# Second attention and feed-forward stage: the quantised second layer moved behind the last exp, two tiles in a turn

## The chip, the cores and the metric

One core of one Trainium2 chip runs the whole program. The metric is the device time of one execution in microseconds (us). Engines are named as in the profile: PE is TensorE, with PEld for its weight loads, DVE is VectorE, ACT is ScalarE, POOL is GpSimd, SP is SyncE, which here only issues DMAs.

## The reference

The reference is four blocks in a row, each added to x with a tanh gate: a perceiver cross-attention, a mixture-of-experts block, a second cross-attention, and a feed-forward block with quantised linear layers. x is 32 x 64 x 128, that is 2048 rows of 128, or NT = 16 tiles of 128 rows. The change lies in the last two blocks, and there in the feed-forward:

```
def act_quant(x):
    scale = 127.0 / clip(max(abs(x), axis=-1), EPS)
    return clip(round(x * scale), -128, 127), scale
...
h = layernorm(x, gamma, beta)          # rows of 128
h = qlinear(h, w1, b1)                 # ternary weights, 128 -> 512
h = gelu(h, approximate=False)
out = qlinear(h, w2, b2)               # quantised again by row, 512 -> 128
```

The second cross-attention (`_L1_xattn_ref`) has 16 heads of 8 and 64 keys for each batch element, so it takes one exp over 16 x 64 scores for each row. The feed-forward takes one gelu over 512 values for each row.

## The kernel before

The program runs in stages one after the other; the last stage, `attention_ffn`, does the last two blocks. It is a software pipeline over the 16 tiles, written out by hand for each engine. Each engine has a loop over turns `s`, and in turn `s` it does one step each for several tiles: for instance ScalarE in turn s does `exp(s - 2)` (line 1609) and `norm_out(s - 5)` (line 1624), VectorE does `row_max(s)` (line 1689), `shift(s - 1)` (line 1694), `attend(s - 2)` (lines 1702 and 1708), `output(s - 2)` (line 1717), `norm_round(s - 4)` (line 1745) and `hidden(s - 5)` (line 1752). Every engine takes its instructions strictly in the order written; semaphores tie the engines together. Whatever stands behind a waiting instruction on its engine waits as well.

The steps of one tile are: turn and project the context and the input on TensorE; `scores` (line 1448) into the four banks `p_s`; row maximum, `shift`, `exp`; `probs_T` (line 1463) turns the probabilities, ScalarE copies them out (`probs_out`, line 1614), `mix` (line 1478) weighs the values; `attend`, `turn_attention`, `attention_out`, `out_proj` and `output` finish the attention. GpSimd normalises the new row, `norm_round` quantises it, `up` (line 1513) is the first ternary layer, and `hidden` scales it back and adds the bias into `hid`, 128 x 512 float32.

The second layer of a tile t is then: `gelu` (ScalarE, line 1628, in place in `hid`), `hidden_largest` (VectorE, row maximum, line 1758), `hidden_factors` (lines 1763 and 1766), `hidden_round` (line 1770), `turn_hidden` (TensorE, four transposes into bank `p_t`, line 1521), `hidden_out` (ScalarE, to bf16, line 1633), `down` (TensorE, four matmuls into `p_y`, line 1530), and `final` (VectorE, line 1777), with `hidden_back` and `add_bias_2` (GpSimd, lines 1387 and 1392) before it. SyncE stores two tiles at a time after `final` (line 1341).

`exp` and `gelu` need different tables of ScalarE, and a table load goes in front of the first of each after the other. So the gelus are taken in groups: `GROUPS` (line 1273) names tiles 0-3, 4-7, 8-11, 12-13 and 14-15, and the gelus of a group run in the turn after the last of its tiles is ready, at the head of ScalarE's turn. `hid` is a ring of eight tiles. The other steps of the second layer lag behind: `hidden_largest` to `hidden_round` run for tile s - 9, `turn_hidden` for s - 11, `down` and `final` for s - 12. `busy` (line 53, its matmuls on line 57) issues matmuls with no use but to keep TensorE at work. `BUSY` (line 1274) puts such calls ahead of `scores` for a few tiles, 5 before tile 9 and 2 before tile 13 among them, and from turn 18 on each turn of TensorE begins with 3 of them, in the lines quoted here. One call is two matmul instructions in the profile.

```
for s in range(NT + 12):
    if s >= NT + 2:
        wait(pe, shifted, NT)
        busy(nc, p_s[:, 0, 0:256], ident[:], v["wq_a"][:, 0:256], 3)
```

Of the kernel before, what the change touches and what calls it, by code (L numbers as in the profile page):

```python
# [22 lines left out]
ALU = mybir.AluOpType  # L23
# [1235 lines left out]
def attention_ffn(nc, v, o_tiles):  # L1259

    xs, cs, moments, neghalf, ident, quad = (v[n] for n in "xs cs moments neghalf ident quad".split())
# [8 lines left out]
    RING = 8  # L1272
    GROUPS = ((0, 4), (4, 8), (8, 12), (12, 14), (14, 16))
    BUSY = {0: 3, 1: 3, 2: 2, 3: 1, 9: 5, 13: 2}
    with ExitStack() as ph, nc.Block() as block:
# [27 lines left out]
        hid = sb("hid", [P, RING, FF])  # L1303
        gT = sb("gT", [P, 2, C, P], BF16)
# [4 lines left out]
        xb2 = sb("xb2", [P, 2, D])  # L1309
# [8 lines left out]
        p_prob, p_mix = (p_m, p_t), (p_m, p_y)  # L1318
# [18 lines left out]
        @block.sync  # L1337
        def _(sp):
            for t in range(NT // 2):
                sp.wait_ge(x_done, 2 * t + 2)  # L1340
                sp.dma_start(o_tiles[:, 2 * t:2 * t + 2, :], xs[:, 2 * t:2 * t + 2, :]).then_inc(stored, 16)
            sp.wait_ge(stored, 16 * (NT // 2))

        @block.gpsimd
        def _(pool):
# [38 lines left out]
            def hidden_back(t):  # L1384
                pool.wait_ge(g_bound, t + 1)
                wait(pool, x_done, t - 3)
                nc.gpsimd.tensor_tensor(back_[:, 1, t % 4], top[:, 1, t % 4], wback[:, 1:2], ALU.mult).then_inc(g_back, 1)

            def add_bias_2(t, tp):
                pool.wait_ge(x_new, t + 1)  # L1390
                wait(pool, x_done, t - 1)
                nc.gpsimd.tensor_tensor(xb2[:, tp, :], xs[:, t, :], rows[:, 3, :], ALU.add).then_inc(xb2_ready, 1)

            pool.wait_ge(ready, 1)
            for s in range(NT + 13):
# [4 lines left out]
                if exists(s - 13, NT):  # L1400
                    add_bias_2(s - 13, (s - 13) % 2)
# [5 lines left out]
                if exists(s - 12, NT):  # L1407
                    hidden_back(s - 12)
# [4 lines left out]
        def _(pe):  # L1413
# [38 lines left out]
            def probs_T(t, tp, j):  # L1452
# [4 lines left out]
                else:  # L1457
                    pe.wait_ge(cT_ready, min(t + 3, NT))
                    wait(pe, gT_ready, t - 8)
# [7 lines left out]
            def mix(t, tp, j):  # L1467
                pe.wait_ge(prT_ready, 2 * t + j + 1)
                pe.wait_ge(v_ready, 2 * t + 2)
                if j == 1:  # L1470
                    wait(pe, x_new, t)
                    wait(pe, hid_ready, t - 3)
                    wait(pe, x_done, t - 9)
# [18 lines left out]
            def out_proj(t, tp):  # L1492
                pe.wait_ge(oT_ready, t + 1)
                wait(pe, hid_ready, t - 2)
                wait(pe, x_done, t - 9)
# [11 lines left out]
            def up(t, tp):  # L1507
# [4 lines left out]
                wait(pe, x_done, t - 6)  # L1512
                nc.tensor.matmul(p_y[:], hT[:, tp, :], w1_t[:], start=True, stop=True).then_inc(up_done, 1)  # L1513

            def turn_hidden(t):
                pe.wait_ge(g_rounded, t + 1)
                pe.wait_ge(cT_ready, min(t + 12, NT))
                pe.wait_ge(prT_ready, min(2 * t + 18, 2 * NT))
                wait(pe, gT_ready, t)
                for c in range(C):  # L1520
                    last = nc.tensor.transpose(p_t[:, c * P:(c + 1) * P], hid[:, t % RING, c * P:(c + 1) * P], ident[:])  # L1521
                last.then_inc(gT_done, 1)

            def down(t, tp):
                pe.wait_ge(gT_ready, t + 1)
                pe.wait_ge(x_new, min(t + 10, NT))
                pe.wait_ge(hid_ready, min(t + 7, NT))
                wait(pe, x_done, t)
                for c in range(C):
                    last = nc.tensor.matmul(p_y[:, 0:D], gT[:, tp, c, :], w2_t[:, c, :], start=(c == 0), stop=(c == C - 1))  # L1530
# [12 lines left out]
            for s in range(NT + 12):  # L1543
                if s >= NT + 2:
                    wait(pe, shifted, NT)
                    busy(nc, p_s[:, 0, 0:256], ident[:], v["wq_a"][:, 0:256], 3)
# [10 lines left out]
                if exists(s - 11, NT):  # L1557
                    turn_hidden(s - 11)
                if exists(s, NT):
                    turn_input(s, s % 2)  # L1560
                if exists(s - 6, NT):
                    up(s - 6, s % 2)
                if exists(s - 3, NT):
# [12 lines left out]
                if exists(s - 12, NT):  # L1576
                    down(s - 12, s % 2)

        @block.scalar
        def _(act):  # L1580
# [45 lines left out]
            def gelu(t):  # L1626
# [214 lines left out]
```

## Time and profile before

| | us |
|---|---|
| median of 3 runs | 463.04 |
| lowest and highest run | 460.96, 463.33 |
| the profiled execution | 460.61 |
| its span, first to last instruction | 458.8 |
| busy in the span: PE, DVE, ACT, POOL | 412.8, 338.7, 263.3, 234.6 |

The span is what the trace covers; 1.8 us of the execution's own time lie around it. The last stage runs from about 304 us to the end. Times in the timeline and in the chain are from the span's start. The granted clock is TensorE's: 1.00 is 2.4 GHz, 0.50 is 1.2 GHz, and a value between is a stretch with both. In the chain of waits each piece is what the piece after it waited for.

### The profile page before, as it was taken

To read this page: it belongs to the slowest core of one execution; us is meant where nothing else is said; L and a number is where in the kernel's file an instruction comes from. 1 tells how busy PE (TensorE), PEld (TensorE's weight loads), DVE (VectorE), ACT (ScalarE), POOL (GpSimd) and SP (SyncE) were. 2 spreads that over 40 slices of the span, in tenths; PEclk is the share of its full clock that TensorE was granted. 3 is DMA by queue.
4 is the path that set the end of the run, shared out by engine and by line. 5 is a ranking of instruction groups with operands and counts; after the bars stand their busy time and mean duration, and the time that the engine had idled before them with its cause. 6 is when DMAs were issued, how large, how long until landed. Compare 5 with 4: busy or idle time off the path is not lost. (4 is left out here: it accounts for less than half of the span.)

```text
span 458.8 us, 11161 instructions
## 1 busy us (share of the span) xinstructions
PE 412.8 (90%) x3810; PEld 307.2 (67%) x3810; DVE 338.7 (74%) x965; ACT 263.3 (57%) x543; POOL 234.6 (51%) x404
## 2 busy tenths in 40 slices
PE   4698999999999999878899989988888979898877
PEld 4355666666666666756788878865666756666656
DVE  3689888888888888865577745553478859879674
ACT  1266777777777776712522244416667768875542
POOL 3545656666666666350300034444388848666621
PEclk8689999999999999999999999989999989988899
DMA  5889999000000000000000000000000000000001
GB/s 166 246 117 120 130 130 106 2 2 2 1 1 3 1 1 2 1 3 0 2 1 0 0 1 2 1 0 2 1 1 3 2 1 1 14 2 15 12 24 34
DMA packets 61285, 13.30 MB, mean 29 GB/s; under 512 B 51488, under 2 KB 60592, under 8 KB 61232
## 3 DMA queue, kind: packets, MB, share of 16 engines
q1 hardware_dynamic: 59776, 11.94, 18.5%
q10 hardware_dynamic: 1328, 0.66, 0.5%
q8 instruction: 32, 0.52, 0.5%
q14 instruction: 21, 0.17, 0.1%
q0 software_dynamic: 128, 0.00, 0.0%
HBM read 11.55 MB, written 1.05 MB: 27 GB/s over the span
## 5 line engine op out<-in xcount | busy, mean ns | idle before, releaser
L332 POOL TENSOR_TENSOR a_rn<-a_ssq,neghalf 128x8 f32<-128x8 f32 x48 | 79.2, 1653 | 25.7 <-DVE a_ssq L682 18.1
L682 DVE TENSOR_REDUCE a_ssq<-a_sq 128x8 f32<-128x512 f32 x48 | 32.4, 675 | 16.1 <-ACT a_sq L539 15.9
L1689 DVE TENSOR_REDUCE b_mx<-b_s 128x16 f32<-128x1024 f32 x16 | 19.6, 1223 | 22.5 <-PE b_s L1448 22.5
L409 PE MATMUL a_x<-wkv_a,a_kvT 128*128 128x512 f32 x64 | 35.3, 634 | 0.5 <-ACT a_kvT L532 0.5
L57 PE MATMUL b_s<-wq_a,ident 128*128 128x256 f32 x106 | 31.9, 448 | 3.1 <-PEq L1139 2.2
L545 ACT ACTIVATE a_vaug<-a_x,maskcol 128x512 f32<-128x512 f32 x32 | 21.9, 683 | 17.8 <-PE a_x L409 17.8
L1355 POOL TENSOR_TENSOR b_k<-b_ksb,quad 128x256 f32<-128x256 f32 x32 | 19.1, 618 | 21.9 <-ACT b_ksb L1595 21.8
L1163 POOL COPY c_staged<-eo_T 128x256 f32<-128x256 f32 x16 | 6.2, 391 | 45.3 <-SPq L1139 44.2
L57 PEld LDWEIGHTS b_s<-wq_a,ident 128*128 128x128 f32 x106 | 22.7, 228 | 6.8 <-issue 2.4
L1100 ACT ACTIVATE e_hg<-e_g 128x512 f32<-128x512 f32 x16 | 9.6, 597 | 28.9 <-PE e_g L1068 28.9
L701 DVE TENSOR_REDUCE a_mx<-a_s 128x4 f32<-128x512 f32 x32 | 22.0, 687 | 3.1 <-PE a_s L435 3.1
L348 POOL TENSOR_TENSOR a_yr<-a_ymv,eps_row 128x1 f32<-128x1 f32 x16 | 3.0, 189 | 41.1 <-DVE a_ymv L725 41.1
L557 ACT ACTIVATE a_kT<-a_m,cols 128x512 f32<-128x512 f32 x32 | 21.9, 686 | 1.4 <-PE a_m L423 1.3
L423 PEld LDWEIGHTS a_m<-ident,a_kn 128*128 128x128 f32 x128 | 15.8, 143 | 9.6 <-issue 8.8
L454 PE MATMUL a_m<-a_vaug,a_prT 128*64 128x65 f32 x512 | 21.9, 228 | 0.3 <-ACT a_prT L567 0.3
L445 PEld LDWEIGHTS a_m<-ident,a_pr 128*128 128x128 f32 x128 | 14.6, 140 | 11.1 <-issue 10.0
L708 DVE TENSOR_TENSOR a_pr<-a_s,a_mx 128x512 f32<-128x512 f32 x32 | 21.9, 684 | 0.0
L435 PEld LDWEIGHTS a_s<-a_kT,a_qT 64*64 64x64 f32 x512 | 13.8, 132 | 12.0 <-issue 12.0
L473 PEld LDWEIGHTS a_y<-wo_a,a_attT 128*128 128x128 f32 x128 | 16.6, 191 | 7.3 <-issue 7.2
L454 PEld LDWEIGHTS a_m<-a_vaug,a_prT 128*64 128x64 f32 x512 | 17.6, 137 | 5.6 <-issue 5.6
L567 ACT COPY a_prT<-a_m 128x512 f32<-128x512 f32 x32 | 18.8, 586 | 4.1 <-PE a_m L445 4.1
L445 PE MATMUL a_m<-ident,a_pr 128*128 128x128 f32 x128 | 20.1, 280 | 0.9 <-ACT a_pr L562 0.9
(254 smaller groups left out, 1237.2 us busy)
## 6 DMA issues: line engine op xcount, KB each, us to landing
w_gu<-in_L_ffn_Wg_dram SPq DMA_DIRECT2D x4, 512.0 KB, 8.7
w_gu<-in_L_ffn_Wu_dram SPq DMA_DIRECT2D x4, 512.0 KB, 11.1
w_d<-in_L_ffn_Wd_dram SPq DMA_DIRECT2D x8, 256.0 KB, 8.1
out_dram<-xs SPq DMA_DIRECT2D x8, 128.0 KB, 1.8
xs<-in_x_dram SPq DMA_DIRECT2D x1, 640.0 KB, 11.4
cs<-in_ctx_dram SPq DMA_DIRECT2D x1, 640.0 KB, 11.8
wkv_a<-in_L_xattn_Wkv_dram SPq DMA_DIRECT2D x1, 512.0 KB, 7.8
nat<-in_L_ffn_w_dram SPq DMA_DIRECT2D x2, 256.0 KB, 2.9
```

The costliest lines, as they stand in the source:

```text
L57: nc.tensor.matmul(bank, weights, moving, start=True, stop=True)
L332: nc.gpsimd.tensor_tensor(rn[:, tp, i, :], ssq[:, tp, i, :], neghalf[:, 0:H0], ALU.pow)\
L409: nc.tensor.matmul(p_x[:], kvT[:, tp, b * 2 * S:(b + 1) * 2 * S], wkv_a[:, INNER:2 * INNER], start=True, stop=True).then_inc(vproj_done, 1)
L445: last = nc.tensor.transpose(p_m[a][:, h * P:(h + 1) * P], pr[:, a, h, :], ident[:])
L454: last = nc.tensor.matmul(p_m[a][b * S:(b + 1) * S, h * W:(h + 1) * W], prT[:, a, h, b * S:(b + 1) * S], vaug[:, tp, b, 2 * h + a, :], sta ...
L545: nc.scalar.activation(vaug[:, tp, b, :, 0:DH0], p_x[:].rearrange("p (h d) -> p h d", h=H0), ACT.Copy, scale=maskcol[:, 2 * t + b:2 * t + ...
L557: nc.scalar.activation(kT[:, tp, b, :, :], p_m[b][:].rearrange("p (h k) -> p h k", h=HP), ACT.Copy, scale=cols[:, 4:5]).then_inc(kT_ready, 1)
L682: nc.vector.tensor_reduce(ssq[:, tp, i, :], sq[:, i, :].rearrange("p (h d) -> p h d", h=H0), AX.X, ALU.add).then_inc(reduced, 1)
L701: nc.vector.tensor_reduce(mx[:, a, :], p_s[a][:].rearrange("p (h k) -> p h k", h=HP), AX.X, ALU.max)\
L708: nc.vector.tensor_tensor(pr[:, a], s3, mx[:, a, :].unsqueeze(2).to_broadcast([P, HP, P]), ALU.subtract).then_inc(shifted, 1)
L1355: last = nc.gpsimd.tensor_tensor(k4[:, tp, b], ksb[:, tp, b].unsqueeze(1).to_broadcast([P, G, S]), quad[:].unsqueeze(2).to_broadcast([P, G ...
L1689: nc.vector.tensor_reduce(mx[:, tp], s4, AX.X, ALU.max).then_inc(maxed, 1)
```

## The change

All gelus and the whole second layer move behind the last `exp`, and are done for two tiles (a pair j, of NP = 8) in a turn. ScalarE does `gelu(j)` in turn 17 + j, right behind `exp` and ahead of its copies, and `hidden_out(j)` at the end of turn 18 + j. VectorE does `hidden_largest(j)`, `hidden_bound(j)` and `hidden_factor(j)` in turn 17 + j, its two `hidden_round` in turn 18 + j, and `final(j)` in turn 20 + j, between `hidden_largest` and the rounds. TensorE does `down(j)` in turn 20 + j and behind it `turn_hidden(j + 1)`; so `turn_hidden(j)` is in turn 19 + j. The eight transposes of a pair go into two of the four banks `p_s`, whose last scores are gone by then, and the two products into `p_t` or `p_m`. `hid` holds all 16 tiles. Two calls of `busy` stand in each `turn_hidden`, ahead of its wait for the rounded rows; the calls for tiles 9 and 13 and those at the head of the late turns are gone, and so are the waits on the second layer in `mix`, `probs_T`, `out_proj`, `up` and `hidden`. The second bias is added in place in `xs`, for two tiles at once.

```
-    RING = 8
-    GROUPS = ((0, 4), (4, 8), (8, 12), (12, 14), (14, 16))
-    BUSY = {0: 3, 1: 3, 2: 2, 3: 1, 9: 5, 13: 2}
+    NP = NT // 2
+    BUSY = {0: 3, 1: 3, 2: 2, 3: 1}
...
-        hid = sb("hid", [P, RING, FF])
-        gT = sb("gT", [P, 2, C, P], BF16)
+        hid = sb("hid", [P, NT, FF])
+        gT = sb("gT", [P, 2, 2, C, P], BF16)
...
-        p_prob, p_mix = (p_m, p_t), (p_m, p_y)
+        p_prob, p_mix, p_out = (p_m, p_t), (p_m, p_y), (p_t, p_m)
...
-                sp.wait_ge(x_done, 2 * t + 2)
+                sp.wait_ge(x_done, t + 1)
...
-            def hidden_back(t):
-                pool.wait_ge(g_bound, t + 1)
-                wait(pool, x_done, t - 3)
-                nc.gpsimd.tensor_tensor(back_[:, 1, t % 4], top[:, 1, t % 4], wback[:, 1:2], ALU.mult).then_inc(g_back, 1)
-            def add_bias_2(t, tp):
-                pool.wait_ge(x_new, t + 1)
-                wait(pool, x_done, t - 1)
-                nc.gpsimd.tensor_tensor(xb2[:, tp, :], xs[:, t, :], rows[:, 3, :], ALU.add).then_inc(xb2_ready, 1)
+            def add_bias_2(j):
+                pool.wait_ge(x_new, 2 * j + 2)
+                pool.wait_ge(mv_ready, 2 * j + 2)
+                r = slice(2 * j, 2 * j + 2)
+                nc.gpsimd.tensor_tensor(xs[:, r, :], xs[:, r, :], rows[:, 3, :].unsqueeze(1).to_broadcast([P, 2, D]),
+                                        ALU.add).then_inc(xb2_ready, 1)
+            def hidden_back(j):
+                pool.wait_ge(g_bound, j + 1)
+                wait(pool, x_done, j - 1)
+                r = slice(2 * (j % 2), 2 * (j % 2) + 2)
+                nc.gpsimd.tensor_tensor(back_[:, 1, r, 0], top[:, 1, r, 0], wback[:, 1:2].to_broadcast([P, 2]),
+                                        ALU.mult).then_inc(g_back, 1)
 
             pool.wait_ge(ready, 1)
-            for s in range(NT + 13):
+            for s in range(NT + 4 + NP):
                 if exists(s - 4, NT):
                     add_bias(s - 4, s % 2)
                 if exists(s - 7, NT):
                     norm_back(s - 7)
-                if exists(s - 13, NT):
-                    add_bias_2(s - 13, (s - 13) % 2)
                 if exists(s - 3, NT):
                     spread_keys(s - 3, (s - 3) % 2)
                 if exists(s - 6, NT):
                     inverse_root(s - 6)
                     norm(s - 6, s % 2)
-                if exists(s - 12, NT):
-                    hidden_back(s - 12)
+                if exists(s - NT - 4, NP):
+                    hidden_back(s - NT - 4)
+                    add_bias_2(s - NT - 4)
...
-            def turn_hidden(t):
-                pe.wait_ge(g_rounded, t + 1)
-                pe.wait_ge(cT_ready, min(t + 12, NT))
-                pe.wait_ge(prT_ready, min(2 * t + 18, 2 * NT))
-                wait(pe, gT_ready, t)
-                for c in range(C):
-                    last = nc.tensor.transpose(p_t[:, c * P:(c + 1) * P], hid[:, t % RING, c * P:(c + 1) * P], ident[:])
+            def turn_hidden(j):
+                if j < 2:
+                    pe.wait_ge(shifted, NT)
+                wait(pe, gT_ready, j - 1)
+                busy(nc, p_s[:, 2 * (j % 2), 0:256], ident[:], v["wq_a"][:, 0:256], 2)
+                pe.wait_ge(g_rounded, 2 * j + 2)
+                for i in range(2):
+                    for c in range(C):
+                        last = nc.tensor.transpose(p_s[:, 2 * (j % 2) + i, c * P:(c + 1) * P],
+                                                   hid[:, 2 * j + i, c * P:(c + 1) * P], ident[:])
                 last.then_inc(gT_done, 1)
 
-            def down(t, tp):
-                pe.wait_ge(gT_ready, t + 1)
-                pe.wait_ge(x_new, min(t + 10, NT))
-                pe.wait_ge(hid_ready, min(t + 7, NT))
-                wait(pe, x_done, t)
-                for c in range(C):
-                    last = nc.tensor.matmul(p_y[:, 0:D], gT[:, tp, c, :], w2_t[:, c, :], start=(c == 0), stop=(c == C - 1))
+            def down(j):
+                pe.wait_ge(gT_ready, j + 1)
+                if j == 0:
+                    pe.wait_ge(prT_ready, 2 * NT)
+                if j == 1:
+                    pe.wait_ge(att_ready, NT)
+                wait(pe, x_done, j - 1)
+                for i in range(2):
+                    for c in range(C):
+                        last = nc.tensor.matmul(p_out[j % 2][:, i * P:(i + 1) * P], gT[:, j % 2, i, c, :], w2_t[:, c, :],
+                                                start=(c == 0), stop=(c == C - 1))
                 last.then_inc(down_done, 1)
...
-            for s in range(NT + 12):
-                if s >= NT + 2:
-                    wait(pe, shifted, NT)
-                    busy(nc, p_s[:, 0, 0:256], ident[:], v["wq_a"][:, 0:256], 3)
+            for s in range(NT + 4 + NP):
                 if exists(s - 1, 2):
                     turn_ternary(s - 1)
                 if s == 3:
@@ -1554,12 +1557,14 @@
                     project(s - 1, (s - 1) % 2)
                 if exists(s - 3, NT):
                     mix(s - 3, (s - 3) % 2, 1)
-                if exists(s - 11, NT):
-                    turn_hidden(s - 11)
                 if exists(s, NT):
                     turn_input(s, s % 2)
                 if exists(s - 6, NT):
                     up(s - 6, s % 2)
+                if exists(s - NT - 4, NP):
+                    down(s - NT - 4)
+                if exists(s - NT - 3, NP):
+                    turn_hidden(s - NT - 3)
...
-                if exists(s - 12, NT):
-                    down(s - 12, s % 2)
...
-            def gelu(t):
-                act.wait_ge(hid_ready, t + 1)
-                nc.scalar.activation(hid[:, t % RING, :], hid[:, t % RING, :], ACT.Gelu).then_inc(gelu_done, 1)
-            def hidden_out(t, tp):
-                act.wait_ge(gT_done, t + 1)
-                wait(act, down_done, t - 1)
-                nc.scalar.activation(gT[:, tp].rearrange("p c k -> p (c k)"), p_t[:], ACT.Copy, bias=-MAGIC)\
-                    .then_inc(gT_ready, 1)
+            def gelu(j):
+                act.wait_ge(hid_ready, 2 * j + 2)
+                pair = hid[:, 2 * j:2 * j + 2, :].rearrange("p t k -> p (t k)")
+                nc.scalar.activation(pair, pair, ACT.Gelu).then_inc(gelu_done, 1)
+            def hidden_out(j):
+                act.wait_ge(gT_done, j + 1)
+                wait(act, down_done, j - 1)
+                nc.scalar.activation(gT[:, j % 2].rearrange("p i c k -> p (i c k)"),
+                                     p_s[:, 2 * (j % 2):2 * (j % 2) + 2, :].rearrange("p i k -> p (i k)"),
+                                     ACT.Copy, bias=-MAGIC).then_inc(gT_ready, 1)
...
-            for s in range(NT + 11):
+            for s in range(NT + 2 + NP):
                 if s == 2:
                     ternary_out(0, w1_t[:])
                 if s == 3:
                     ternary_out(1, w2_t[:].rearrange("p c k -> p (c k)"))
-                for first, end in GROUPS:
-                    if s - 7 == end - 1:
-                        for t in range(first, end):
-                            gelu(t)
                 if exists(s, NT):
                     context_out(s, s % 2)
                 if exists(s - 1, NT):
                     projections_out(s - 1, (s - 1) % 2)
                 if exists(s - 2, NT):
                     exp(s - 2, s % 2)
+                if exists(s - NT - 1, NP):
+                    gelu(s - NT - 1)
                 if exists(s, NT):
                     input_out(s, s % 2)
-                if exists(s - 11, NT):
-                    hidden_out(s - 11, (s - 11) % 2)
...
+                if exists(s - NT - 2, NP):
+                    hidden_out(s - NT - 2)
...
-            def hidden_largest(t):
-                dve.wait_ge(gelu_done, t + 1)
-                wait(dve, g_back, t - 3)
-                nc.vector.tensor_reduce(top[:, 1, t % 4], hid[:, t % RING, :], AX.X, ALU.max, apply_absolute_value=True)\
-                    .then_inc(g_max, 1)
-            def hidden_factors(t):
-                dve.wait_ge(g_max, t + 1)
-                nc.vector.tensor_scalar(top[:, 1, t % 4], top[:, 1, t % 4], EPS, 1.0 / 127.0, ALU.max, ALU.mult)\
+            def pair(j):
+                return slice(2 * (j % 2), 2 * (j % 2) + 2)
+            def hidden_largest(j):
+                dve.wait_ge(gelu_done, j + 1)
+                wait(dve, g_back, j - 1)
+                nc.vector.tensor_reduce(top[:, 1, pair(j), 0], hid[:, 2 * j:2 * j + 2, :], AX.X, ALU.max,
+                                        apply_absolute_value=True).then_inc(g_max, 1)
+            def hidden_bound(j):
+                dve.wait_ge(g_max, j + 1)
+                nc.vector.tensor_scalar(top[:, 1, pair(j), 0], top[:, 1, pair(j), 0], EPS, 1.0 / 127.0, ALU.max, ALU.mult)\
                     .then_inc(g_bound, 1)
-                dve.wait_ge(g_bound, t + 1)
-                nc.vector.reciprocal(fine[:, 1, t % 4], top[:, 1, t % 4]).then_inc(g_fine, 1)
+            def hidden_factor(j):
+                dve.wait_ge(g_bound, j + 1)
+                nc.vector.reciprocal(fine[:, 1, pair(j), 0], top[:, 1, pair(j), 0]).then_inc(g_fine, 1)
 
             def hidden_round(t):
-                dve.wait_ge(g_fine, t + 1)
-                nc.vector.tensor_scalar(hid[:, t % RING, :], hid[:, t % RING, :], fine[:, 1, t % 4], MAGIC,
+                dve.wait_ge(g_fine, t // 2 + 1)
+                nc.vector.tensor_scalar(hid[:, t, :], hid[:, t, :], fine[:, 1, t % 4], MAGIC,
                                         ALU.mult, ALU.add).then_inc(g_rounded, 1)
 
-            def final(t, tp):
-                dve.wait_ge(down_done, t + 1)
-                dve.wait_ge(xb2_ready, t + 1)
-                dve.wait_ge(g_back, t + 1)
-                nc.vector.scalar_tensor_tensor(xs[:, t, :], p_y[:, 0:D], back_[:, 1, t % 4], xb2[:, tp, :],
-                                               ALU.mult, ALU.add).then_inc(x_done, 1)
-            for s in range(NT + 12):
+            def final(j):
+                dve.wait_ge(down_done, j + 1)
+                dve.wait_ge(xb2_ready, j + 1)
+                dve.wait_ge(g_back, j + 1)
+                for i in range(2):
+                    last = nc.vector.scalar_tensor_tensor(xs[:, 2 * j + i, :], p_out[j % 2][:, i * P:(i + 1) * P],
+                                                          back_[:, 1, (2 * j + i) % 4], xs[:, 2 * j + i, :],
+                                                          ALU.mult, ALU.add)
+                last.then_inc(x_done, 1)
+            for s in range(NT + 4 + NP):
                 if exists(s - 3, NT):
                     row_stats(s - 3, (s - 3) % 2)
-                if exists(s - 12, NT):
-                    final(s - 12, s % 2)
                 if exists(s - 1, NT):
                     shift(s - 1, (s - 1) % 2)
                 if exists(s - 3, NT):
                     row_moments(s - 3, (s - 3) % 2)
                 if exists(s - 2, NT):
                     attend(s - 2, s % 2)
-                if exists(s - 9, NT):
-                    hidden_largest(s - 9)
+                if exists(s - NT - 1, NP):
+                    hidden_largest(s - NT - 1)
                 if exists(s - 4, NT):
                     norm_round(s - 4, s % 2)
-                if exists(s - 9, NT):
-                    hidden_factors(s - 9)
+                if exists(s - NT - 4, NP):
+                    final(s - NT - 4)
+                if exists(s - NT - 2, NP):
+                    hidden_round(2 * (s - NT - 2))
+                if exists(s - NT - 1, NP):
+                    hidden_bound(s - NT - 1)
                 if exists(s - 5, NT):
                     hidden(s - 5)
-                if exists(s - 9, NT):
-                    hidden_round(s - 9)
+                if exists(s - NT - 2, NP):
+                    hidden_round(2 * (s - NT - 2) + 1)
+                if exists(s - NT - 1, NP):
+                    hidden_factor(s - NT - 1)
...
```

## Rows read from the trace of the kernel before

**Rows 1.** The page of the profiled execution, its head

```profile
span 458.8 us, 11161 instructions
```

**Rows 2.** Timeline of ScalarE: start, duration, engine, line, operation, idle before it.

```profile
343.60 1.06 ACT L1609 ACTIVATE b_pr<-b_pr 128x1024 f32<-128x1024 f32 x1
...
361.78 1.06 ACT L1609 ACTIVATE b_pr<-b_pr 128x1024 f32<-128x1024 f32 x1
...
380.01 1.06 ACT L1609 ACTIVATE b_pr<-b_pr 128x1024 f32<-128x1024 f32 x1
...
393.08 1.06 ACT L1609 ACTIVATE b_pr<-b_pr 128x1024 f32<-128x1024 f32 x1
...
396.57 1.28 ACT L1628 ACT_TABLE_LOAD   x1
397.87 2.19 ACT L1628 ACTIVATE b_hid<-b_hid 128x512 f32<-128x512 f32 x4
...
409.82 1.06 ACT L1609 ACTIVATE b_pr<-b_pr 128x1024 f32<-128x1024 f32 x1
...
422.40 1.06 ACT L1609 ACTIVATE b_pr<-b_pr 128x1024 f32<-128x1024 f32 x1 [2.57 <-DVE b_pr L1694]
```

**Rows 3.** Busy time of the engines in five stretches, with the granted clock.

```profile
core 0: us, PE busy (x) PEld busy (x) DVE busy (x) ACT busy (x) POOL busy (x), PEclk, DMA share, GB/s
343.60:361.80 18.20, 15.85 (x213) 12.11 (x213) 15.69 (x44) 13.05 (x34) 14.86 (x31) 1.00 0.01 3
418.00:422.00 4.00, 2.78 (x47) 2.44 (x47) 3.78 (x10) 1.68 (x5) 2.89 (x7) 1.00 0.00 0
422.00:425.50 3.50, 3.50 (x19) 2.80 (x16) 3.13 (x12) 2.49 (x4) 2.62 (x6) 0.51 0.03 7
428.00:432.00 4.00, 2.81 (x27) 1.63 (x25) 3.04 (x11) 2.98 (x7) 2.45 (x6) 1.00 0.11 33
432.20:435.40 3.20, 3.19 (x11) 2.55 (x12) 1.78 (x8) 0.00 (x0) 2.13 (x5) 0.51 0.00 0
```

**Rows 4.** The chain that ended last, its last stage: start, duration, what.

```profile
422.14 1.04 PE b_t L1521 x4
...
448.57 1.35 PE b_s L57 x6
449.93 0.44 PE b_t L1521 x4
450.36 0.22 PE b_y L1530 x4
...
456.22 0.35 DVE xs L1777
```

**Rows 5.** Timeline of all engines in the tail: start, duration, engine, line, operation.

```profile
429.26 0.21 DVE L1708 TENSOR_TENSOR b_att<-b_y,b_rs 128x64 f32<-128x64 f32 x1
...
443.17 0.75 DVE L1752 SCALAR_TENSOR_TENSOR b_hid<-b_y,b_back_,b1row 128x512 f32<-128x512 f32 x1 [0.67 <-PE b_y L1513]
...
443.83 0.48 DVE L1770 TENSOR_SCALAR b_hid<-b_hid,b_fine 128x512 f32<-128x512 f32 x1
444.14 0.24 PEld L1530 LDWEIGHTS b_y<-w_t,b_gT 128*128 128x128 bf16 x4 [1.40 <-ACT b_gT L1633]
...
450.40 0.60 ACT L1633 ACTIVATE b_gT<-b_t 128x512 bf16<-128x512 f32 x1 [1.41 <-PE b_t L1521]
```

**Rows 6.** Groups of the last stage by shape: busy, mean ns, idle before.

```profile
L1689 DVE TENSOR_REDUCE b_mx<-b_s 128x16 f32<-128x1024 f32 x16 | 19.6, 1223 | 22.5 <-PE b_s L1448 22.5
...
L1355 POOL TENSOR_TENSOR b_k<-b_ksb,quad 128x256 f32<-128x256 f32 x32 | 19.1, 618 | 21.9 <-ACT b_ksb L1595 21.8
...
L1758 DVE TENSOR_REDUCE b_top<-b_hid 128x1 f32<-128x512 f32 x16 | 10.8, 674 | 0.0
...
L1614 ACT COPY b_prT<-b_t 128x512 f32<-128x512 f32 x16 | 9.5, 592 | 0.2 <-PE b_t L1463 0.2
```

**Rows 7.** The instructions of line 1770: durations in ns, min/median/max, first and last start.

```profile
L1770 DVE TENSOR_SCALAR b_hid<-b_hid,b_fine x16: 476/479/794, 369.5 to 452.0; 128x512 f32<-128x512 f32 x16
```

More of the change, by code:

```diff
@@ L1308, in attention_ffn @@
         wback = sb("wback", [P, 2])
-        xb2 = sb("xb2", [P, 2, D])
         wscale = sb("wscale", [P, 2])
@@ L1458, in probs_T @@
                     pe.wait_ge(cT_ready, min(t + 3, NT))
-                    wait(pe, gT_ready, t - 8)
                     wait(pe, prT_ready, 2 * t)
@@ L1472, in mix @@
                     wait(pe, hid_ready, t - 3)
-                    wait(pe, x_done, t - 9)
                     wait(pe, att_ready, t)
@@ L1494, in out_proj @@
                 wait(pe, hid_ready, t - 2)
-                wait(pe, x_done, t - 9)
                 nc.tensor.matmul(p_y[:, 0:D], oT[:, tp, :], w_c[:, 3, :], start=True, stop=True).then_inc(y_done, 1)
@@ L1511, in up @@
                 wait(pe, hid_ready, t)
-                wait(pe, x_done, t - 6)
                 nc.tensor.matmul(p_y[:], hT[:, tp, :], w1_t[:], start=True, stop=True).then_inc(up_done, 1)
-            def turn_hidden(t):
-                pe.wait_ge(g_rounded, t + 1)
-                pe.wait_ge(cT_ready, min(t + 12, NT))
-                pe.wait_ge(prT_ready, min(2 * t + 18, 2 * NT))
-                wait(pe, gT_ready, t)
-                for c in range(C):
-                    last = nc.tensor.transpose(p_t[:, c * P:(c + 1) * P], hid[:, t % RING, c * P:(c + 1) * P], ident[:])
-                last.then_inc(gT_done, 1)
-            def down(t, tp):
-                pe.wait_ge(gT_ready, t + 1)
-                pe.wait_ge(x_new, min(t + 10, NT))
-                pe.wait_ge(hid_ready, min(t + 7, NT))
-                wait(pe, x_done, t)
-                for c in range(C):
-                    last = nc.tensor.matmul(p_y[:, 0:D], gT[:, tp, c, :], w2_t[:, c, :], start=(c == 0), stop=(c == C - 1))
+            def turn_hidden(j):
[8 more added lines that the diff above has]
+                                                   hid[:, 2 * j + i, c * P:(c + 1) * P], ident[:])
+                last.then_inc(gT_done, 1)
+            def down(j):
[9 more added lines that the diff above has]
+                                                start=(c == 0), stop=(c == C - 1))
                 last.then_inc(down_done, 1)
@@ L1750, in hidden @@
                 dve.wait_ge(h_back, t + 1)
-                wait(dve, gT_done, t - RING + 1)
-                nc.vector.scalar_tensor_tensor(hid[:, t % RING, :], p_y[:], back_[:, 0, t % 4], b1row[:],
+                nc.vector.scalar_tensor_tensor(hid[:, t, :], p_y[:], back_[:, 0, t % 4], b1row[:],
                                                ALU.mult, ALU.add).then_inc(hid_ready, 1)
-            def hidden_largest(t):
-                dve.wait_ge(gelu_done, t + 1)
-                wait(dve, g_back, t - 3)
-                nc.vector.tensor_reduce(top[:, 1, t % 4], hid[:, t % RING, :], AX.X, ALU.max, apply_absolute_value=True)\
-                    .then_inc(g_max, 1)
```

## The prediction

> **What bounds the kernel now.** I read four views, and only for the last stage, since the change touches no other. The span is 458.8 us [rows 1], and the profiled execution took 460.61, so 1.8 lie around the span. The sum below is made against this execution; it is 2.4 us (0.5%) under the median of 463.04. About 0.5% is also what a measurement of this kernel can tell from no change.
>
> The timeline of ScalarE [rows 2] gives the pace. From the exp at 343.60 to that at 361.78 lie three turns: 6.06 us each, with TensorE busy 15.85 of 18.20 us at a granted clock of 1.00 [rows 3]. From there to the exp of the last tile at 422.40 lie eight turns in 60.62 us, or 7.6 each. The reader is to see where the excess over 6.06 sits: 6.1 us in the two turns to 380.01 (the first group of gelus and the cold turn behind it), 1.0 in the two turns to 393.08 (the first `down`), 4.6 in the two to 409.82 (a load of 1.28, four gelus in 2.19, and a second load, all ahead of ScalarE's copies), 0.5 in the last two. Together 12.1.
>
> After the last exp comes the tail, 34.2 us from 422.40 to the end of the last `final` at 456.57 [rows 2, 4]; the store of the last rows takes 2.2 more. The chain of waits there is all TensorE: for a tile 1.35 of `busy`, 0.44 of four transposes, 0.22 of `down`, 2.01 in sum [rows 4]. The filler sets the pace, and the rest hides behind it.
>
> **What the change takes away.** The eight turns lose the gelus, four of the six table loads, the two extra fillers and the second layer. What is left is the turn of 343.60 to 361.78, which already ran without any of these and stayed at clock 1.00. So the last exp starts at 361.78 + 8 x 6.06 = 410.3, a gain of 12.1. Transposes and row work that leave these turns give nothing beyond this: the turn of 6.06 was paced without them. The waits on the second layer that go from `mix`, `probs_T`, `out_proj` and `up` are priced at nothing of their own, since in the turn of 6.06 they did not yet wait for anything. SyncE keeps its eight stores; each goes as soon as its pair is done, and only the last counts, 2.2 as before.
>
> **What it adds: a ring through four engines.** In the tail I wrote down, engine by engine, the order of the instructions. VectorE in turn 18 + j: `hidden_largest(j+1)`, `final(j-2)`, round, bound, round of pair j. The row maximum needs `gelu(j+1)`. ScalarE takes `gelu(j+1)` only behind `hidden_out(j-1)`, the last item of its turn before. That needs `turn_hidden(j-1)`, and that the rounds of pair j-1, the turn before on VectorE. So from round to round everything stands in one line, with two tiles for each trip. The new wait of `hidden_out` at the head of ScalarE's queue is the knot: the next gelu is ready to run, and is queued behind it.
>
> One trip, step by step:
> - VectorE to TensorE 0.22: a `hidden` of 0.75 started at 443.17, so it ended at 443.92, and the weight load that it let go started at 444.14 [rows 5].
> - Eight transposes: four are 0.44 in the chain [rows 4], the last result about 0.16 later; 8 x 0.11 + 0.16 = 1.04.
> - TensorE to ScalarE 0.03 (chain piece ends 450.37, `hidden_out` starts 450.40), then `hidden_out` over 1024 elements. 512 took 0.60 and the exp over 1024 took 1.06 [rows 2, 5], so 1.05.
> - `gelu(j+1)`, the pair in one instruction: four of 512 took 2.19 [rows 2], 0.53 for each further one, so 1.06, less 0.08 of overlap: 0.98, and 0.05 to VectorE.
> - `hidden_largest` over 1024: 512 took 0.674, and the row maximum over 1024 from PSUM 1.223 [rows 6]. VectorE starts the next instruction 0.09 before one ends (443.17 + 0.75 against 443.83 [rows 5]), so 1.13.
> - `final` twice, 0.35 each [rows 4], 0.27 in a row: 0.54. First round 0.40, bound 0.16 (estimate from the smallest operations), second round 0.48 [rows 7].
>
> Sum: 0.22 + 1.04 + 0.03 + 1.05 + 0.98 + 0.05 + 1.13 + 0.54 + 0.40 + 0.16 + 0.48 = 6.1 us for a pair, where two tiles took 4.02. Off the ring lie `down`, `busy`, factor, GpSimd and the stores: TensorE does `down` and the filler while it would wait.
>
> Two terms the trace of before does not show as such. **GpSimd beside the rounds:** `final` lets `hidden_back` and `add_bias_2` go, the latter over 256 elements, about 0.6 us like line 1355 [rows 6], and they fall on the rounds. Line 1770 took 479 ns as a rule and up to 794 [rows 7]. The bounds are 0 and 0.3 for each of two rounds; I take 0.16 for a trip. The Trainium skill, SBUF — State Buffer, "Who interferes with whom", says that VectorE in a two-port mode and GpSimd exclude each other for a whole instruction. By this rule the price would be the whole rest of a GpSimd instruction each time; the spread of line 1770 agrees with it.
>
> **TensorE's clock:** in a trip of 6.1 us TensorE has some 2.7 us of work: 1.04 of transposes, 0.6 of `down`, 1.0 of filler, 44% busy. In 418.0 to 422.0 it was busy 2.78 of 4.00 us, and 422.0 to 425.5 then ran at 0.51; in 428 to 432 it was 2.81 of 4.00, and 432.2 to 435.4 ran at 0.51 [rows 3]. Both were busier than a trip of the ring. So I expect 1.2 GHz for most of the tail. There four transposes take 1.04 on the chain in place of 0.44 [rows 4]; twice that difference is 1.2 for eight. I take +0.8, since the piece of 1.04 holds the start of the first transpose, which eight pay once; the ends are 0 and +1.2. The Trainium skill, TensorE: Matmul & The Clock Gate, Part 4, says that transposes do not count as work for the clock in the way that matmuls do. By that the tail is at 1.2 GHz whatever the two fillers do. The turns at clock 1.00, with a dozen transposes each, show that they at least do not prevent it.
>
> **The tail in full,** from the last exp at 410.3, cold values in brackets.
> - Up to the end of `attend` for the last tile: exp 1.06, load 1.28, gelu(0) 1.06, `attention_out` 0.3, two `probs_out` 1.1 (line 1614, 592 ns [rows 6]), `mix` 0.65, `attend` 0.65: 6.1. These stand in line, as gelu(0) is ahead of the copies. Before, `attend` ended 7.1 after the exp [rows 2, 5], so the load hurts little here.
> - Two turns of VectorE with a row maximum, `hidden`, the norm's and the output's work each, about 3.3 (3.13 to 3.78 us of its work stood in 3.5 to 4.0 before [rows 3]): 6.6. The rounds of pair 0 are done at 410.3 + 12.7 = 423.0.
> - Six trips: 36.6, plus two `hidden` and a norm left over (1.5), less one `final` (0.5), plus 1.0 for GpSimd: 38.6 (+4.9).
> - Behind the sixth: transposes, `hidden_out`, `down`, filler, transposes of pair 7, `hidden_out`, `down`, two `final`: 7.5 (10.4).
>
> So the last `final` ends at 423.0 + 38.6 + 7.5 = 469.1, or 476.9 cold. With the store's 2.2 and 1.8 around the span: 473.1, or 480.9. The tail has become 59 to 67 us in place of 34.2, against 12.1 gained. I take 480, the cold case with a few trips at full clock.
>
> **Rivals.**
> - *The tail stays at 2.4 GHz*, as the fillers mean it to: 473. For it: eight pieces of work in a trip leave no long gap. Against: the two stretches above. Chance 0.25.
> - *The steps overlap, and it is faster.* If the rounds of a pair did not stand behind the next row maximum, a trip would be VectorE's own work, 2.7 + 0.16, or 2.9 us, the six trips 19.4, and the time 473.1 - 19.2 = 454. The point from which this decides is a trip of 4.2 us: 12.7 + 6 x 4.2 + 1.0 + 7.5 = 46.4 = 34.2 + 12.1. The ring is 1.9 above it, and only an error in the order of a queue, not in a duration, could bring it there. Chance 0.04. The Trainium skill, ScalarE: Activation LUTs, "Table sets: the hidden batching unit", asks for just this change: all calls of one table set together. By the rule alone, four loads of 1.28 us, about 5 us, are gained; the trace agrees that each load is there, and it is inside the 12.1.
> - *The change does only part of what it says:* without the second layer the turns do not fall to 6.06, because something else, such as the clock, holds them at 6.7. Then 480 + 5 = 485. Against: the three turns at 1.00. Chance 0.1.
> - The forecast itself, 480 within 3: 0.61.
>
> **Range and chances.** Warm and cold tail are 473 and 481; the unknown costs add 2 below (lead-in) and 4 above (transposes, GpSimd), and the slow turns reach 485. I give 471 to 488. Faster by over 0.5%: 0.04. Within 0.5%: 0.02. Slower: 0.94.
>
> **What would show it.** Right: exps 6.1 apart up to one at about 410; then `hidden_out` 6 to 7 us apart, each row maximum starting right behind a gelu, each gelu right behind a `hidden_out`, ScalarE idle until TensorE's transposes and VectorE idle until the gelu, TensorE at 0.50 or little more from about 425 on. Wrong: pairs 3 to 4 us apart with VectorE busy throughout; or exps that keep 6.7 and more; or a chain with `busy` on it in the tail.

## The result and the profile after

The changed kernel takes 479.29 us (median of 4 runs, 478.68 to 479.61), against 462.00 for the kernel before in the same comparison: a ratio of 1.0376, 95% interval 1.0331 to 1.042. The forecast was 480, in a range of 471 to 488. Ratios, here and below, are of the means of the executions, without the few that fell in a slower state of the chip; the times given are medians. The profiled execution has a span of 476.9 us, and all the readings in this section are of it.

| from the start of the span, us | before | forecast | after |
|---|---|---|---|
| exp of tile 7 starts | 361.78 | 361.78 | 361.53 |
| exp of the last tile starts | 422.40 | 410.3 | 409.20 |
| its `attend` ends | 429.47 | 416.4 | 416.34 |
| rounds of pair 0 end | | 423.0 | 423.5 |
| last `final` ends | 456.57 | 469.1 warm, 476.9 cold | 474.65 |

The tail, from the start of the last exp to the end of the last `final`, takes 65.5 us in place of 34.2.

The first view is ScalarE's timeline again; it answers to [rows 2].

```profile
409.20 1.06 ACT L1612 ACTIVATE b_pr<-b_pr 128x1024 f32<-128x1024 f32 x1 [2.00 <-DVE b_pr L1697]
410.27 1.28 ACT L1632 ACT_TABLE_LOAD   x1
...
425.56 1.02 ACT L1637 ACTIVATE b_gT<-b_s 128x1024 bf16<-128x1024 f32 x1 [6.87 <-PE b_s L1522]
426.48 1.05 ACT L1632 ACTIVATE b_hid<-b_hid 128x1024 f32<-128x1024 f32 x1
...
431.99 1.02 ACT L1637 ACTIVATE b_gT<-b_s 128x1024 bf16<-128x1024 f32 x1 [4.30 <-PE b_s L1522]
...
445.16 1.02 ACT L1637 ACTIVATE b_gT<-b_s 128x1024 bf16<-128x1024 f32 x1 [4.52 <-PE b_s L1522]
...
452.37 1.02 ACT L1637 ACTIVATE b_gT<-b_s 128x1024 bf16<-128x1024 f32 x1 [5.24 <-PE b_s L1522]
453.29 1.05 ACT L1632 ACTIVATE b_hid<-b_hid 128x1024 f32<-128x1024 f32 x1
...
459.58 1.02 ACT L1637 ACTIVATE b_gT<-b_s 128x1024 bf16<-128x1024 f32 x1 [5.24 <-PE b_s L1522]
...
472.30 1.02 ACT L1637 ACTIVATE b_gT<-b_s 128x1024 bf16<-128x1024 f32 x1 [4.50 <-PE b_s L1522]
```

The last eight turns up to the exp at 409.20 take 5.96 us on average: all the excess of before is gone. From one `hidden_out` (L1637) to the next, over all eight of them, are 6.43, 6.69, 6.48, 7.21, 7.21, 7.20 and 5.52 us. ScalarE has been idle for 6.87 us ahead of the first of them and for 4.3 to 5.2 us ahead of each other one, waiting for the transposes. As soon as it has one, it takes the gelu (L1632) that stood behind.

The chain of waits shows one whole trip, from the transposes of a pair to those of the next:

```profile
450.37 1.98 PE b_s L1522 x8
452.40 0.90 issue
453.29 1.06 ACT b_hid L1632
454.37 0.06 DVE b_top L1763
454.44 1.07 issue
455.51 0.60 DVE xs L1785 x2
456.11 0.39 DVE b_hid L1777
456.50 0.08 DVE b_top L1768
456.58 0.95 DVE b_hid L1777
457.53 0.04 issue
```

Read down: transposes, `hidden_out` (the piece "issue" of 0.90, since the gelu starts 0.92 after it), gelu, row maximum (0.06 and the "issue" of 1.07), the two finals, first round, bound, second round. From 450.37 to the next transposes at 457.57 are 7.20. TensorE, ScalarE and VectorE are on it in turn, and each stands idle while the others work. In the kernel before, the chain lay on TensorE alone only from 444.2 on; in the 15 us ahead of that VectorE's `hidden` (L1752, 0.76 each) stood on it as well.

In the first trip the ring was not what came last. The filler of TensorE was, behind `down`:

```profile
428.36 0.85 PE b_t L1535 x8
429.21 1.81 PE b_s L57 x4
431.02 0.95 PE b_s L1522 x8
```

It stood on the chain once more, for 1.81 again, ahead of the transposes of the last pair (468.89), and nowhere else.

The windows view says at what clock, as [rows 3] did before:

```profile
core 0: us, PE busy (x) PEld busy (x) DVE busy (x) ACT busy (x) POOL busy (x), PEclk, DMA share, GB/s
363.60:403.85 40.25, 34.90 (x475) 27.00 (x472) 34.87 (x97) 28.47 (x74) 31.37 (x66) 1.00 0.01 2
409.20:425.50 16.30, 11.26 (x64) 8.15 (x64) 10.52 (x38) 6.38 (x10) 10.09 (x22) 0.54 0.01 2
425.50:438.70 13.20, 8.95 (x45) 6.53 (x43) 6.33 (x15) 4.30 (x7) 0.98 (x2) 0.66 0.03 11
438.70:445.20 6.50, 2.79 (x20) 1.95 (x20) 3.21 (x7) 1.98 (x3) 0.98 (x2) 0.96 0.07 20
445.20:472.30 27.10, 18.85 (x80) 14.25 (x80) 11.55 (x27) 6.90 (x7) 4.16 (x8) 0.51 0.09 25
```

The attention turns stay at 1.00. The tail is at 0.54, 0.66, 0.96 and 0.51; in the stretch at 0.96 the pair took 6.48, in the last one a full trip took 7.2.

### The profile page after: what moved, and what is told of

The parts are those of the page before. It is cut to its first block and busy times, and to the rows that moved or that the text cites. A ratio compares the mean times of both kernels' runs of the same rounds, so it can differ in the third digit from the quotient of the medians.

```text
span 476.9 us, 10923 instructions
## 1 busy us (share of the span) xinstructions
PE 413.4 (87%) x3768; PEld 305.4 (64%) x3768; DVE 339.3 (71%) x941; ACT 257.3 (54%) x523; POOL 232.6 (49%) x388
## 5 line engine op out<-in xcount | busy, mean ns | idle before, releaser
L1637 ACT ACTIVATE b_gT<-b_s 128x1024 bf16<-128x1024 f32 x8 | 8.2, 1024 | 40.4 <-PE b_s L1522 40.4
L1354 POOL TENSOR_TENSOR b_k<-b_ksb,quad 128x256 f32<-128x256 f32 x32 | 19.0, 614 | 19.2 <-ACT b_ksb L1598 19.2
L57 PE MATMUL b_s<-wq_a,ident 128*128 128x256 f32 x64 | 23.0, 504 | 3.1 <-PEq L1139 2.2
L1763 DVE TENSOR_REDUCE b_top<-b_hid 128x2 f32<-128x1024 f32 x8 | 9.7, 1214 | 21.1 <-ACT b_hid L1632 21.1
```

The source lines that it names most:

```text
L57: nc.tensor.matmul(bank, weights, moving, start=True, stop=True)
L1354: last = nc.gpsimd.tensor_tensor(k4[:, tp, b], ksb[:, tp, b].unsqueeze(1).to_broadcast([P, G, S]), quad[:].unsqueeze(2).to_broadcast([P, G ...
```

## The experiments

Each kernel is the changed one with the edit shown. The times are medians beside runs of the kernel before on the same chip: 461.48 us for the order of ScalarE, the five calls of `busy`, the early bias and the late `final`; 460.36 for the kernel without `busy` and for the last one of the table; 461.57 for the rest. Executions differ by some us ahead of the edits (the last exp starts between 408.7 and 414.1), so the tail of the profiled one, from the last exp's start to the end of the last `final`, is given too: it is 65.5 us in the changed kernel.

**One line on ScalarE.** `hidden_out` goes one turn later, so that it stands behind the next gelu and not ahead of it:

```
-                if exists(s - NT - 2, NP):
-                    hidden_out(s - NT - 2)
+                if exists(s - NT - 3, NP):
+                    hidden_out(s - NT - 3)
```

> Ring theory: with hidden_out(j-1) behind gelu(j+1) in place of ahead of it, the round trip spans two turns of VectorE instead of one. The pace of a pair falls from 6.4 to 7.2 us to VectorE's own work, about 3.4 (row maximum 1.13, two finals 0.6, rounds 1.4, the small ones 0.3), the chain in the tail runs over VectorE, and the kernel takes 457 to 462 us. Rival, cold clock or size of the work: the pairs are slow because TensorE is at 1.2 GHz and GpSimd stands beside the rounds, the order of ScalarE's queue is not what counts: the pace stays above 6, the time within 1% of 479.

Measured: 459.62 us, a ratio to before of 0.998 (0.9936 to 1.0025). By the medians this one line gives back 19.7 us (18 by the ratios), the whole loss of 17.3; a difference to the kernel before is not shown. The tail fell from 65.5 to 46.3. GpSimd still stands beside the second round (1.03 us) and the work in the tail is the same. TensorE's clock did rise with it, from 0.61 to 0.78 over the tail, so this run alone does not rule out the cold clock; the next one does, with a clock of 0.86 and a tail of 62.7. The pace was 3.53, and the chain of the late tail is not VectorE's, against what I expected:

```profile
438.56 1.03 ACT b_gT L1637
...
439.64 0.62 PE b_m L1535 x8
440.26 0.92 PE b_s L57 x4
441.18 0.89 PE b_s L1522 x8
442.09 1.03 ACT b_gT L1637
```

It goes from `hidden_out` (L1637) over `down` (L1535) and the filler (L57) to the next pair's transposes (L1522): a second, shorter ring, made by the order on TensorE.

**The clock.** Five calls of `busy` in `turn_hidden`, or none, in place of two (`..., 2)` becomes `..., 5)` or `..., 0)`).

> Five calls of busy in each turn_hidden in place of two. Ring theory: TensorE has idle time in each trip, so the calls cost nothing, and the granted clock stays at 1.00; the eight transposes take 1.3 in place of 2.0 us, trips become 6.45 in place of 7.2, and the last stretch of two turns shortens as well or loses a little to the longer filler: 474 to 477 us. Rival, the ring is not the limit: no gain, or the filler itself comes on the chain, 479 to 486.

> The changed kernel without the two calls of busy in turn_hidden. If they do not hold the clock, the granted clock is 0.5 in the whole tail, the trips are 7.2 us from the first to the last (a little less where the filler stood on the chain, 1.8 us in the first full trip and 1.8 in the last), and the time stays within 2 us of 479. If they do hold it in part (pairs 2 to 4 ran at 6.4 to 6.7), it is lost there: 480 to 482. A theory in which the filler itself slows the tail gives 473 or less.

Measured: 476.40 us with five (ratio to before 1.0329, 1.0242 to 1.0415; tail 62.7) and 482.12 with none (1.0455, 1.039 to 1.0521; tail 66.1). The windows, of the kernel with five and then of that with none:

```profile
core 0: us, PE busy (x) PEld busy (x) DVE busy (x) ACT busy (x) POOL busy (x), PEclk, DMA share, GB/s
425.70:439.70 14.00, 9.76 (x57) 7.92 (x55) 6.33 (x15) 4.27 (x6) 0.98 (x2) 0.88 0.03 10
439.70:469.90 30.20, 19.42 (x131) 15.51 (x130) 14.76 (x34) 8.92 (x10) 5.13 (x10) 1.00 0.09 27
```

```profile
core 0: us, PE busy (x) PEld busy (x) DVE busy (x) ACT busy (x) POOL busy (x), PEclk, DMA share, GB/s
425.00:475.00 50.00, 23.35 (x123) 18.71 (x124) 22.79 (x55) 13.16 (x15) 8.27 (x18) 0.50 0.06 16
```

With five calls the last full trips ran at 1.00 and took 6.33; with none the tail ran at 0.50 and they took 7.27. So the clock is worth about 0.9 us a trip, and the ring is there at either clock. The 5.7 us between the two kernels are not the clock's price: 2.3 of them lie ahead of the last exp (409.48 and 411.75), and the tails differ by 3.4 only, as the filler itself came on the chain with five calls. It stood there for 3.72 us in the trip from 431.92 to 439.75, which took 7.83. Two calls held the clock now and then.

**GpSimd beside the rounds.** `add_bias_2` moves into the attention turns:

```
                     norm(s - 6, s % 2)
+                if s % 2 == 1 and exists((s - 7) // 2, NP):
+                    add_bias_2((s - 7) // 2)
...
                     hidden_back(s - NT - 4)
-                    add_bias_2(s - NT - 4)
```

> add_bias_2 is done on GpSimd in the attention turns, one pair every second turn, behind the norm of its second tile, in place of the tail. If it is the instruction that holds up the second round (1.02 us in place of 0.48), the second round falls to 0.5 to 0.7, each trip by 0.3 to 0.5, six trips by 2 to 3 us: 476 to 477, unless the attention turns get longer. Rival: the second round is slow for another reason (the small product of hidden_back alone, or waiting for its own pipeline): it stays at 1.0, and the time at 479.

VectorE and GpSimd in the changed kernel, and then VectorE's rounds in this one:

```profile
448.82 0.48 DVE L1777 TENSOR_SCALAR b_hid<-b_hid,b_fine 128x512 f32<-128x512 f32 x1
449.05 0.30 POOL L1395 TENSOR_TENSOR b_back_<-b_top,b_wback 128x2 f32<-128x2 f32 x1 [5.51 <-DVE xs L1785]
...
449.28 1.03 DVE L1777 TENSOR_SCALAR b_hid<-b_hid,b_fine 128x512 f32<-128x512 f32 x1
449.31 0.72 POOL L1388 TENSOR_TENSOR xs<-xs,rows 128x256 f32<-128x256 f32 x1
```

```profile
448.60 0.47 DVE L1778 TENSOR_SCALAR b_hid<-b_hid,b_fine 128x512 f32<-128x512 f32 x1
...
449.06 0.48 DVE L1778 TENSOR_SCALAR b_hid<-b_hid,b_fine 128x512 f32<-128x512 f32 x1
```

In the first, the second round (L1777, at 449.28) takes 1.03 and ends 0.28 after GpSimd's addition does (L1388, 449.31 + 0.72); in the second it takes 0.48. The small product of `hidden_back` (L1395) is still beside the rounds there, so it is the addition that holds the second one up. That is so in four trips of the changed kernel; in the first ones `hidden` (L1754) stands between the two rounds on VectorE, and the second one, coming later, takes 0.48. The time was inconclusive: 479.04, but in four executions from 475.88 to 480.10, with mean granted clocks of 0.934 down to 0.917. In the profiled one, of 475.88, the tail was 62.3, and the later trips were 5.8 us where the clock was high and 6.7 where it was low, each 0.5 to 0.7 under those of the changed kernel. The shorter trip seems to have met the low clock more often in the others; that is not shown, as they have no trace.

**`final` behind the rounds** on VectorE (the two lines of `final` move behind `hidden_factor`).

> final(j) moves on VectorE behind the rounds and the factor, where VectorE waits for the next gelu anyway. Ring theory: every trip loses the two finals, 0.6 us, so six or seven trips give 3.5 to 4; and what final lets go on GpSimd starts behind the rounds, so the second round falls to 0.5 as well, another 3. Together 472 to 474. Rival, throughput: VectorE's work is the same and the time stays at 479.

Measured: 474.97 us (ratio 1.0287, 1.0198 to 1.0376). In the trace the trips fell to 5.3 to 5.5 us:

```profile
454.63 1.02 ACT L1637 ACTIVATE b_gT<-b_s 128x1024 bf16<-128x1024 f32 x1 [3.57 <-PE b_s L1522]
...
459.90 1.02 ACT L1637 ACTIVATE b_gT<-b_s 128x1024 bf16<-128x1024 f32 x1 [3.30 <-PE b_s L1522]
```

That is 1.7 to 1.9 less than 7.2, and more than the two terms I had named (0.6 and 0.55), since the clock came up too: 0.87 from 444 to 470. Against the 6.33 of a trip at 1.00, the 5.27 are 1.06 less, which is near the two terms. The tail took 57.4 us in place of 65.5. Half of that gain did not reach the time of this execution, as its first turns of the stage were slower, far ahead of the edit (the last exp starts at 413.69).

**The gelu behind the probabilities' copies** (the two lines of `gelu` move behind `probs_out(s - 2, 1)`).

> The changed kernel with this one edit (gelu behind the copies of the last probabilities). The ring theory says that the pace of the pairs stays at 6.4 to 7.2 us, since within a trip gelu(j+1) still stands behind hidden_out(j-1): 478 to 479. A rival, that the table load ahead of the copies is what makes the tail long, would give 474 or less.

Measured: 477.50 us (ratio 1.0376, 1.0295 to 1.0457). `attend` of the last tile ended 5.5 us after the exp's start in place of 7.1, but the trips stayed at 6.3 to 7.2. Where the load stands is not what makes the tail long.

**Breaking the rings one after the other.** On TensorE `turn_hidden(s - NT - 3)` goes ahead of `down(s - NT - 4)`, on top of the first edit; then `add_bias_2` early as well; then also the late gelu, or also the late `final`.

> As e1_order, and on TensorE turn_hidden(j+1) goes ahead of down(j). In e1_order the chain of the late tail is hidden_out(j), down(j), busy, turn_hidden(j+1), hidden_out(j+1): 1.03 + 0.05 + 0.62 + 0.92 + 0.89 = 3.53 us for a pair, a shorter ring. Ring theory: with this ring broken too, the pace falls to VectorE's own work, 3.3 us with the slow second round: only 0.2 us for a pair, some 1 to 1.5 us in all, 458 to 459. Rival: the pace of 3.53 in e1_order is VectorE's already (its steps sum to 3.3 and the rest is waiting for semaphores): no change.

> As e5_turn_first, with add_bias_2 in the attention turns. If the pace is VectorE's now, the second round's fall from 1.03 to 0.48 goes through to every pair: 2.8 to 2.9 us, some 4 to 5 us under e1_order: 454 to 456, faster than the kernel before by 1% or more. Rival: another ring of 3.4 to 3.5 us holds the pace, and the time stays at 458 to 459.

> As e6_best, with the gelu of a turn behind the copies of the last probabilities, so that the table load and gelu(0) no longer stand ahead of them. If the lead-in waits for these copies, attend of the last tile ends 1.3 to 1.5 us sooner, and the time falls by 1 us (453 to 455). Rival: the lead-in is set by VectorE's chain of two turns and by gelu(0) itself: no change, or a little slower.

> As e6_best, and final goes behind the rounds on VectorE. In e6_best the chain of the late tail is a third, shorter ring: transposes of pair j+1 1.09, down(j) 0.46, final(j) 0.61, rounds 0.87, 3.10 us with the latencies. With final behind the rounds it is broken, and what is left is VectorE's own work of 2.85 us. Ring theory: 0.25 us for each of six pairs, 1 to 1.5 in all: 453 to 454. Rival: VectorE was already within a tenth of its own work, and the last final comes later by its place: no change, 454 to 455.

| kernel | us | ratio to before | pace of a late pair | tail |
|---|---|---|---|---|
| order of ScalarE alone | 459.62 | 0.998 (0.9936 to 1.0025) | 3.53 | 46.3 |
| and `turn_hidden` first | 458.92 | 0.9943 (0.9904 to 0.9982) | 3.65 | 43.7 |
| and the bias early | 454.79 | 0.9892 (0.9805 to 0.9978) | 3.10 | 41.4 |
| and the gelu late | 455.23 | 0.9864 (0.9804 to 0.9925) | 3.10 | 40.9 |
| bias early and `final` late | 455.99 | 0.9885 (0.9843 to 0.9926) | 3.10 | 41.2 |

The third kernel is about 1% faster than the kernel before. By the times it is not clearly apart from the second, whose interval overlaps its own; its tail is 2.3 us shorter. The last three can't be told apart by their times. The pace of the third is not VectorE's own work (2.85) either; its chain:

```profile
440.74 1.09 PE b_s L1523 x8
441.83 0.46 PE b_t L1536 x8
442.32 0.61 DVE xs L1786 x2
442.93 0.40 DVE b_hid L1778
443.32 0.07 DVE b_top L1769
443.40 0.40 DVE b_hid L1778
443.84 1.09 PE b_s L1523 x8
```

Transposes (L1523), `down` (L1536), the finals that wait for it (L1786), the rounds (L1778), the next transposes: a third ring, through `final` ahead of the rounds. It was there in the kernel above it too, with the slow second round in it, 3.65; my 3.3 for that one was wrong, and its total right only because its first two trips (3.87 and 3.02 in place of 6.05 and 3.53) and its last one got shorter. Moving `final` back broke this ring, and a fourth took its place at the same 3.10, which I had not seen:

```profile
443.36 0.52 DVE xs L1786 x2
...
444.01 0.21 POOL b_back_ L1395
...
444.31 1.22 DVE b_top L1764
445.53 0.40 DVE b_hid L1778
```

`final` (L1786) lets `hidden_back` go on GpSimd (L1395), and the next row maximum (L1764) waits for that, as `top` and `back_` have room for two pairs only. More room was not tried. The late gelu brought 0.5 us of tail here, which the times do not show: `attend` ended 5.0 us after the exp's start in place of 6.2, but the row maximum then waited 0.32 for gelu(0).

## Why the prediction was right

- **The gain ahead of the tail.** Forecast: eight turns of 6.06, the last exp at 410.3. Measured 409.20: seven turns of about 6.05 and a last one of 5.35. The step that says that the second layer paid for all the excess held.
- **The ring.** This was the step on which the sign hung, and the one-line edit shows it (it runs through three engines, not four as its heading in the prediction has it; GpSimd only holds up a round on it): the same work in another order on one queue has a tail 19.2 us shorter. The trip was forecast at 6.1 warm and 6.9 cold, with 0.16 for GpSimd on top of each. Measured: 6.33 warm and 7.2 to 7.27 cold. The six trips together took 41.2, between the 38.6 and 43.5 of the two forecasts, and what came behind them 9.9, between 7.5 and 10.4.
- **The terms of the trip.** Transposes were put at 1.04 and, cold, 0.8 more; the chain has 1.11 with the clock at 1.00 (five calls of `busy`) and 1.98 at 0.51. The 0.16 in the first of these had no row behind it. From VectorE to TensorE I put 0.22 and it was 0.04. **GpSimd was mis-sized**: 0.16 for a trip, and in four of the six trips the second round took 0.55 more than 0.48, 2.2 us in all against 1.0. That is inside my bound of 0.6 for a trip, but outside the 0.3 for one round; even the longest case of line 1770, 794 ns [rows 7], was 0.32 over its usual 0.48. These errors cancelled in part, which was luck.
- **The rule on the shared port.** The Trainium skill (SBUF — State Buffer, "Who interferes with whom") says that of VectorE in a two-port mode and GpSimd, the one that comes second waits for the whole of the first's instruction. By that rule, the trace agrees in the main: here the round lasted until 0.28 after GpSimd's addition, and was back at 0.48 without it. A full round behind the addition would have ended 0.2 later still. I should have priced it by a whole GpSimd instruction, 0.72, and would have been 0.17 over.
- **The clock.** Forecast: 1.2 GHz for most of the tail. Measured 0.54, 0.66, 0.96, 0.51 in its stretches. It was low already ahead of the 425 that I had named. That two calls would not hold it came true, but the sentence that the tail is at 1.2 GHz whatever the fillers do is too strong: with five calls, and the same transposes, it ran at 1.00. The rival of a warm tail, 473, became a run: 476.4, where part of the filler stood on the chain. The clock was the smaller part: 0.9 us a trip, an estimate of some 6 us for six trips, against 19 for the order.
- **The filler.** I put it off the ring, and named a chain with `busy` on it in the tail as a sign of being wrong. The chain had it twice, 1.81 each: in the last turns, where the sum had it too, and in the first trip, where it had not. From the second trip on it was off the chain, as forecast.
- **The lead-in.** Forecast 12.7 from the exp's start to the rounds of pair 0, measured 14.3. `attend` ended after 7.1 and not 6.1: I had counted one `mix`, at 0.65, and two stood in a row on TensorE, 0.98 and 0.88 at half clock. VectorE's two turns took 7.2 and not 6.6. That the exp came 1.1 sooner offset most of this, by luck.
- **A reading that was wrong.** The chain of the kernel before was not "all TensorE": from about 430 to 444 it had `hidden` of VectorE on it. The sum does not use it.
- **The rival on the other side** had its mechanism right as well: with the steps overlapped the kernel does come out faster than before, at 454.8, where 454 was forecast for a pace of 2.9. But it takes three edits to the changed kernel to get there, and the pace is 3.1. The 454 also counts GpSimd's 1.0 twice, in the pace and on top of it, so that its nearness is partly luck.

## What to carry to other kernels

When engines take their instructions strictly in order, write down for each engine what stands ahead of what in one turn, and follow the waits around: a step that waits for this turn's product, put ahead of the step that starts the next, closes a ring, and the pace is then the sum of its latencies and not the busiest engine's work. The chain of the first ring here shows no wait for a free buffer, and one line in another order opened it; the last one found is made by room for two pairs, and whether more room would open that was not tried. Breaking one ring uncovers the next, so read the chain again after each edit: here the second edit shortened the tail by 2.6 us and still left a slower late pace, 3.65 after 3.53.

## What the runs showed of the hardware

- A VectorE `tensor_scalar` over 128 x 512 float32 in SBUF took 0.48 us alone and 1.02 to 1.03 beside two GpSimd instructions of 0.30 and 0.72, ending 0.28 after the second of them. Where the rounds stood first, in the last pair of the changed kernel, it was GpSimd's addition that took longer, 0.97 in place of 0.72 (at 465.70).
- Eight float32 transposes of 128 x 128 stood on the chain for 1.11 us at a granted clock of 1.00 and for 1.98 at 0.51.
- The busy share that the profile gives for TensorE was no guide to its clock: 18.85 of 27.10 us went with a granted clock of 0.51 in the changed kernel, and 19.42 of 30.20 with 1.00 in the one with five calls of `busy`. A part of this is that the same matmuls last longer at 1.2 GHz and so look busier.
- In the profiled executions a shorter trip went with a higher clock, without any more filler. Over the tail it was 0.61 in the changed kernel, 0.73 with `final` moved, 0.78 with ScalarE's order and 0.83 in the third kernel of the table, so that an edit gave more than its own term. It is no rule: with the early bias alone it was 0.64, and of the whole execution it was 0.934 there and down to 0.917 in others of the same kernel.
